# Delta attention: a semaphore for each producer, a place for each step, and waits set again from the data

## The chip, the cores and the metric

The kernel runs on one core of a Trainium2 chip. The metric is the device time of one execution in microseconds. The core has five engines with queues of their own: TensorE (PE), VectorE (DVE), ScalarE (ACT), GpSimd (POOL) and SyncE (SP, which only starts DMAs here). They meet only through semaphores: an instruction raises one when it ends, and another engine's queue, or the same engine's, waits until it has reached a number.

## What is computed

The kernel computes a small model of four layers (attention and feed-forward in each). The change lies in the attention of the first layer, a gated delta rule with 16 heads of 128, two batches and 1,024 tokens:

```python
q = short_conv(x @ Wq.T, conv_q); k = short_conv(x @ Wk.T, conv_k); v = short_conv(x @ Wv.T, conv_v)
v_hat = einsum('bthk,vk->bthv', k, Wsv); e = v_hat - v
s = stack([s_l2, s_l1, s_cos], -1)
beta = sigmoid(_mlp(s, Wb1, bb1, Wb2, bb2)); amp = _mlp(s, Wa1, ba1, Wa2, ba2)
g = -exp(A_log) * softplus(k / norm(k) * amp + dt_bias)
def step(S, inp):
    q_t, k_t, v_t, g_t, b_t = inp
    S = S * exp(g_t)[..., None]
    kv = einsum('bhk,bhkv->bhv', k_t, S)
    delta = (v_t - kv) * b_t[..., None]
    S = S + k_t[..., None] * delta[..., None, :]
    o_t = einsum('bhk,bhkv->bhv', q_t * scale, S)
    return (S, o_t)
o = o * rsqrt(mean(o * o, -1, keepdims=True) + NORM_EPS) * norm_w * sigmoid(x @ Wg1.T @ Wg2.T + bg2)
return o.reshape(Bsz, Tlen, NH * DV) @ Wo.T
```

Here short_conv is a causal convolution over 4 tokens with a silu behind it, and s holds three numbers of how far v_hat is from v.

## The kernel before

`delta_attention` cuts the work into 64 units u: head u // 4, and of the head's 2,048 tokens a group of 512 (`tok`). Units 0 and 1 of a head (`first(u)`) begin the two batches, units 2 and 3 go on with them: they take over three columns of the projections (`tail`) and the state St. A unit passes through the engines like this, by the lines of the kernel before:

- PE projects k, v and q (L301), ACT copies them out scaled by the last tap (L533 the three columns of the tail, L534 the rest), DVE adds the other taps (L723, three times each for k, v and q). In units 2 and 3 of a head three small multiplications `early` (L871), a sum L873 and an addition L876 bring in the tail. ACT puts the silu on all three (L587), DVE rounds tiny numbers away (L860 k, L862 v, L878 q).
- PE turns v (L352), multiplies k by Wsv (L360), ACT and DVE square and multiply (L579 to L581, L621 to L623, L757, L852), PE sums over channels (L345) and turns the sums (L475). DVE takes them out (L750 to L752), POOL takes roots (L685, L686, L687), and the small MLPs run on POOL (L682, L705 to L708, L697, L698), ACT (L570, L636) and DVE (L766 to L770, L787, L832 to L834, L906 to L908). PE spreads their results over the channels (L367, L373), DVE forms z (L845), ACT and DVE the softplus (L626 to L630, L824, L740, L842) and ACT the decay (L574).
- Seven levels lv turn 128 tokens of a chunk into one triangular solve. At each, PE multiplies keys with scaled keys and queries (`products`, L312 for levels 0 to 4, L318 for 5 and 6), POOL scales keys and queries for the next level (`scale`: L666 kq, L667 kF, L668 tot), DVE copies the products under a mask (`mask`, L737), PE multiplies blocks (`in_blocks`, L325), ACT copies the result (Xs, L591) and DVE subtracts it (TB, L886).
- The recurrence goes over 4 chunks k: PE multiplies the state St (L394), DVE forms R (L796), PE multiplies (L433), ACT copies Dl (L607), PE adds up state and output (L463, L467, L470), and DVE renews St (L896 in the first chunk of a batch, L898 in the others).
- The output is squared (ACT L596) and gated (DVE og, L840), PE sums the squares (L508), DVE and POOL make the root (L817, L703), PE multiplies by Wo (L424) and DVE adds to x (L783).

The units overlap. A slot g runs from 0 to 7 x 63 + 33; a step with the offset off works on unit (g - off) / 7 where that is whole (`at`). The order of the `if` blocks in an engine's part, slot after slot, is the order of its queue: it is written out by hand, and an engine carries out its queue strictly in this order. Some ten steps share counters: `scaled`, `masked` and `p_mm` count all seven levels, `rounded` is raised only by the last of three roundings. Where an engine's instruction needs the result of the one ahead of it, `ch.link` (class Chain) puts a wait right behind the producer, so that the next instruction in the queue waits, whichever it is.

## Time and profile before

| | before |
|---|---|
| median of 3 runs | 6105.31 us (6090.98 to 6112.95) |
| span of the profiled execution | 6108.1 us |
| PE busy in it | 5563.4 us, 91% |
| DVE, ACT, POOL busy | 3399.1 us (56%), 2691.6 us (44%), 1937.6 us (32%) |
| first and last power L685 on POOL, 64 in all | 64.6 and 2568.1 us |

The share of busy time is over all nine stages of the program; the stage of this change ends soon after the last L685. A row of a timeline tells when an instruction (or several like it in a row, xN) began and how long it lasted, with, in square brackets, how long its engine had been idle and who ended that. An instruction that begins before its neighbour's end overlaps with it in the engine's pipeline.

### The profile page before, as it was taken

What the parts mean: (1) busy time and instruction counts of PE and PEld (TensorE: products, weight loads), DVE (VectorE), ACT (ScalarE), POOL (GpSimd) and SP (SyncE); (2) the same over time, 40 slices, a digit from 0 to 9 for tenths busy, and PEclk for the clock granted to TensorE, in tenths of its full rate; (3) what the DMA queues carried; (4) which work ended last, traced back from release to release, by engine and by line L of the source; (5) the groups of instructions that cost most, each with busy time, mean ns of one, the idle gap of its engine ahead of it and who ended that gap; (6) DMA issues with size and microseconds to landing.
All of it is one profiled execution on the core that took longest, in us unless ns stands there. A gap on an engine that the chain in (4) does not pass through costs nothing. (4 is left out here: it accounts for less than half of the span.)

```text
span 6108.1 us, 162699 instructions
## 1 busy us (share of the span) xinstructions
PE 5563.4 (91%) x69266; PEld 3711.6 (61%) x69266; DVE 3399.1 (56%) x7451; ACT 2691.6 (44%) x5744; POOL 1937.6 (32%) x2352
## 2 busy tenths in 40 slices
PE   5888888888888888889999999899989899999999
PEld 3666656666665666656777776533336667767665
DVE  5677777777777777633444443386624444444322
ACT  4555555555555555513555553236651222222211
POOL 3666666666666666610000000110000011111000
PEclk7999999999999999979999999989999999999999
DMA  0000000000000000000000000000010112111100
GB/s 28 7 7 7 7 7 7 7 7 7 7 7 3 7 7 7 3 17 12 15 11 11 15 10 23 7 1 1 1 56 1 37 67 67 67 67 67 63 7 7
DMA packets 34317, 116.15 MB, mean 19 GB/s; under 512 B 4416, under 2 KB 9792, under 8 KB 33600
## 3 DMA queue, kind: packets, MB, share of 16 engines
q1 hardware_dynamic: 33600, 105.74, 5.1%
q8 instruction: 553, 9.06, 0.6%
q14 instruction: 164, 1.34, 0.1%
HBM read 103.63 MB, written 2.10 MB: 17 GB/s over the span
## 5 line engine op out<-in xcount | busy, mean ns | idle before, releaser
L666 POOL TENSOR_TENSOR d_kq<-d_kq,d_tot 128x512 f32<-128x512 f32 x448 | 558.6, 1247 | 788.1 <-PE d_lpd L312 635.2
L723 DVE SCALAR_TENSOR_TENSOR d_qkv<-d_fr,d_wts,d_qkv 128x509 f32<-128x509 f32 (+2 forms) x576 | 428.3, 744 | 81.7 <-ACT d_qkv L534 72.6
L301 PE MATMUL d_fr<-xnT,d_wts 128*128 128x512 f32 x768 | 404.0, 652 | 9.4 <-DMA d_wts<-in_headw 5.2
L1845 DVE TENSOR_REDUCE r_nm<-r_ps 128x2 f32<-128x1024 f32 x256 | 307.8, 1223 | 138.7 <-PE r_ps L1664 138.6
L1943 PE MATMUL e_pj<-xnT,e_wts 128*128 128x512 f32 x768 | 347.9, 602 | 13.9 <-DMA e_wts<-in_w3all 12.2
L1059 POOL TENSOR_TENSOR f1rstd<-f1var,mhalf 128x4 f32<-128x4 f32 x4 | 4.0, 1010 | 1090.1 <-DVE f1var L1084 1090.1
L1765 ACT ACTIVATE r_pT<-r_ps 128x512 f32<-128x512 f32 x512 | 274.9, 598 | 146.3 <-PE r_ps L1672 145.8
L667 POOL TENSOR_TENSOR d_kF<-d_kF,d_tot 128x256 f32<-128x256 f32 x448 | 316.8, 707 | 0.0
L1296 PEld LDWEIGHTS c_po<-c_pT,c_vt 128*128 128x128 f32 x2304 | 294.7, 191 | 21.0 <-ACT c_pT L1361 9.3
L1296 PE MATMUL c_po<-c_pT,c_vt 128*128 128x128 f32 x2304 | 301.9, 276 | 0.2
L1664 PE MATMUL r_ps<-r_kT,r_qT 32*128 32x512 f32 x1024 | 291.5, 690 | 2.7 <-DVE r_nm L1845 1.1
L1251 PE MATMUL c_sc<-c_kT,c_qT 128*128 128x512 f32 (+3 forms) x768 | 290.2, 487 | 0.7 <-ACT c_qT L1322 0.7
L1399 DVE TENSOR_TENSOR c_sc<-c_sc,c_mask 128x128 f32<-128x128 f32 x256 | 76.7, 300 | 382.6 <-PE c_sc L1251 382.6
L1672 PE MATMUL r_ps<-r_qT,r_kT 32*128 32x512 f32 x1024 | 278.6, 648 | 0.8 <-ACT r_pT L1765 0.8
L685 POOL TENSOR_TENSOR d_pw<-d_st,d_half 128x20 f32<-128x20 f32 x64 | 250.0, 3907 | 71.5 <-DVE d_sums L752 71.5
L995 PE MATMUL f3pg<-xnT,f3ws 128*128 128x512 f32 x544 | 246.2, 595 | 6.9 <-DMA f3ws<-in_f3w 6.9
L1943 PEld LDWEIGHTS e_pj<-xnT,e_wts 128*128 128x128 f32 x768 | 141.2, 191 | 178.1 <-issue 153.1
L591 ACT ACTIVATE d_Xs<-d_xy 128x128 f32<-128x128 f32 (+1 forms) x384 | 111.3, 290 | 280.6 <-PE d_xy L325 269.4
L534 ACT ACTIVATE d_qkv<-d_fr,d_wts 128x512 f32<-128x512 f32 x192 | 131.8, 686 | 212.8 <-PE d_fr L301 212.0
L433 PE MATMUL d_ca<-d_R,d_TT 128*128 128x128 f32 x512 | 130.6, 339 | 92.7 <-DVE d_R L796 83.9
L301 PEld LDWEIGHTS d_fr<-xnT,d_wts 128*128 128x128 f32 x768 | 138.2, 200 | 125.2 <-issue 104.5
L2074 POOL TENSOR_TENSOR e_acc<-e_acc,e_osq 128x512 f32<-128x512 f32 x60 | 76.1, 1268 | 434.1 <-ACT e_osq L2043 434.1
(437 smaller groups left out, 13527.8 us busy)
## 6 DMA issues: line engine op xcount, KB each, us to landing
e_wts<-in_w3all SPq DMA_DIRECT2D x64, 897.0 KB, 4.6
...
```

Of the source, the lines that this page charges most:

```text
L301: last = nc.tensor.matmul(fr[:, bank, :], w_of(u)[:, w0 + kd * P:w0 + (kd + 1) * P], T.xnT[:, kd, tok(u):tok(u) + GRP], start=(kd == 0), s ...
L666: nc.gpsimd.tensor_tensor(v, v, bc(bc(t_l[:, :, 0], 2, h), 1, 2), ALU.mult)
L667: nc.gpsimd.tensor_tensor(f, f, bc(t_l[:, :, 1], 2, h), ALU.mult)
L685: ch.link(nc.gpsimd.tensor_tensor(pw[:, u % 3], st[:, u % 2], bc(half[:].to_broadcast([P, 5]), 2, NC), ALU.pow))
L723: step = nc.vector.scalar_tensor_tensor(into, fr[:, x // 2, 0:GRP - 3 + i], tap(u, x, i), into, ALU.mult, ALU.add)
L1251: last = nc.tensor.matmul(sc[:, n % 2, k, 0:w], qT[:, h % 2, t * P:(t + 1) * P], kT[:, h // 4 % 2, k * GRP:k * GRP + w], start=True, stop= ...
L1296: last = nc.tensor.matmul(po[:, 0:P], vt[:, n // (4 * QT) % 2, j], pT[:, n % 2, j * P:(j + 1) * P], start=(j == 0), stop=(j == t))
L1664: last = nc.tensor.matmul(ps[:, r + w, :], qT[band(i0 + w), j, tok(t)], kT[band(i0 + w), j // 2, keys], start=True, stop=True, tile_positi ...
L1672: nc.tensor.matmul(ps[:, k, :], kT[band(i), jj // 2, tok(b * QT + kt)], qT[band(i), jj, (G - 1) * GRP:G * GRP], start=True, stop=True, til ...
L1765: nc.scalar.activation(pT[:, N % 3, i, :], ps[:, k, :], ACT.Exp).then_inc(cols_read, 1)
L1845: nc.vector.tensor_reduce(nm[:, t % 2, half, 4 * j + i0:4 * j + i0 + 2], ps[:, row_pair(row - 1):row_pair(row - 1) + 2], AX, ALU.max).then ...
L1943: last = nc.tensor.matmul(pj[:, x % 2, :], w[:, w0 + kd * P:w0 + (kd + 1) * P], T.xnT[:, kd, g * GRP:(g + 1) * GRP], start=(kd == 0), stop ...
```

## The change

The arithmetic stays, and nearly all of the order. Three things change.

The slots become turns: TURNS is 68, and in turn t a step with the offset off (0 to 4) works on unit t - off (`unit`). Each engine's part is one turn of its queue written out, so that each step has a place of its own. PE, POOL and SP keep their order. On DVE the mask of level 1 moves, in units with `early` steps, from behind them to behind the first of them. On ACT the evacuation of k moves ahead of the copy of its tail, in units that have one.

Each producer has its own semaphore, and shared counters go: `scaled_kF[lv]` is raised by L667's successor, `round_k`, `round_v` and `round_q` by the three roundings, `st_floor` by that of L751, `p_mm[lv]`, `yt_mm[lv]` and so on by level. Waits are set anew: one stands where the data needs it and no earlier wait in the queue covers it; many are left only for the first or the last units. Chain has a second form, `did(instruction, name)` and later `after(name)`, which puts the wait ahead of the instruction that needs the result. In the program as built, PE's rows carry 7,353 waits before and 4,316 after, DVE's 7,017 and 4,459, ACT's 4,712 and 3,764, POOL's 1,936 and 1,289. One wait is new: ACT's Abs of sqs 5 waits for the Square that reads it.

The core of the diff:

```diff
+    def did(self, instruction, *step):
         instruction.then_inc(self.sem, 1)
         self.n += 1
+        self.at[step] = self.n
         return self.n
+
+    def after(self, *step):
+        self.need(self.at[step])
 
...
-
-
-def at(g, off):
-    u, r = divmod(g - off, SL)
-    return u if r == 0 and 0 <= u < NU0 else None
+
+
+def unit(t, off):
+    return t - off if 0 <= t - off < NU0 else None
 
```

PE, the transposes of v, the spreads of a1 and rb, and products (of all levels but the first) that wait for kF:

```diff
-                        pe.wait_ge(conv[0], u + 1)
-                        pe.wait_ge(rounded, u + 1)
...
+                        pe.wait_ge(round_v, u + 1)
                         for j in range(NC):
...
+                        pe.wait_ge(rb_ready, u + 1)
+                        for j in range(NC):
+                            last = nc.tensor.transpose(fr[:, 2, ch_(j)], rb[:, j:j + 1].to_broadcast([P, P]), T.ident[:])
+                        last.then_inc(rb_mm, 1)
...
+                    if (u := unit(t, 2)) is not None:
+                        pe.wait_ge(scaled_kF[2], u + 1)
+                        products(u, 3).then_inc(p_mm[3], 1)
```

ACT, the new wait, and k's evacuation; DVE, og, the mask of level 1 and the `early` steps, R of chunk 1; POOL, the scaling:

```diff
+                            act.wait_ge(*w_loaded(u))
+                        act.wait_ge(proj_k, u + 1)
+                        nc.scalar.activation(qkv[:, u % 3, 1], fr[:, 0, :], ACT.Copy, scale=tap(u, 1, 3)).then_inc(evac_k, 1)
+                        if first(u):
+                            if u == 0:
+                                act.wait_ge(tail_set, 1)
+                            nc.scalar.activation(tail[:, u % 2, 1, 0:3], fr[:, 0, GRP - 3:], ACT.Copy).then_inc(tail_k, 1)
...
+                        act.wait_ge(cross_ready, u + 1)
+                        nc.scalar.activation(sqs[:, 2], fr[:, 3, :], ACT.Square)
+                        ch.did(nc.scalar.activation(sqs[:, 3], sqs[:, 5], ACT.Square), "err_sq", u)
+                        ch.after("err_sq", u)
+                        nc.scalar.activation(sqs[:, 5], sqs[:, 5], ACT.Abs).then_inc(err_abs, 1)
...
-                    t_l = tot[:, u % 2, tot_at[lv]:tot_at[lv] + segs].rearrange("p (m two) -> p m two", two=2)
-                    t_n = tot[:, u % 2, tot_at[lv + 1]:tot_at[lv + 1] + segs // 2]
-                    f = even(kF[:, u % 2], h)
...
-                        pool.wait_ge(scaled, 7 * u + lv)
                     v = kq[:, u % 2].rearrange("p x (m two h) -> p x m two h", two=2, h=h)[:, :, :, 1]
-                    nc.gpsimd.tensor_tensor(v, v, bc(bc(t_l[:, :, 0], 2, h), 1, 2), ALU.mult)
-                    nc.gpsimd.tensor_tensor(f, f, bc(t_l[:, :, 1], 2, h), ALU.mult)
-                    nc.gpsimd.tensor_tensor(t_n, t_l[:, :, 0], t_l[:, :, 1], ALU.mult).then_inc(scaled, 1)
...
+                def scale_kF(u, lv):
+                    f = even(kF[:, u % 2], 1 << lv)
+                    return nc.gpsimd.tensor_tensor(f, f, bc(by_pair(u, lv)[:, :, 1], 2, 1 << lv), ALU.mult)
...
+                        ch.did(scale_tot(u, 5), "scaled_tot[5]", u)
+                    if (u := unit(t, 1)) is not None:
+                        pool.wait_ge(st_floor, u + 1)
+                        nc.gpsimd.tensor_tensor(pw[:, u % 3], st[:, u % 2], bc(half[:].to_broadcast([P, 5]), 2, NC), ALU.pow).then_inc(roots, 1)
+                        pool.wait_ge(roots, u + 1)
...
+                        scale_kq(u, 1)
+                        scale_kF(u, 1).then_inc(scaled_kF[1], 1)
+                        ch.did(scale_tot(u, 1), "scaled_tot[1]", u)
+                        ch.after("scaled_tot[1]", u)
...
+                    if (u := unit(t, 4)) is not None:
+                        dve.wait_ge(osq_ready, u + 1)
+                        nc.vector.scalar_tensor_tensor(og[:], tg[:, u % 2], 1.0, co[:], ALU.add, ALU.mult)
...
+                        nc.vector.tensor_scalar(st[:, u % 2, 4], sv[:, 0, :, 0], 1e-24, None, ALU.max).then_inc(st_floor, 1)
...
+                        nc.vector.tensor_tensor(c3(TB[:, 1]), bc(eye[:], 1, NC), c3(xy[:, 0:P]), ALU.subtract)
+                    if (u := unit(t, 0)) is not None:
+                        if not first(u):
+                            nc.vector.tensor_tensor(early[:, :, :, 0], tail[:, u % 2, :, 0:3], bc(taps(u)[:, :, 0], 2, 3), ALU.mult)
+                    if (u := unit(t, 2)) is not None:
+                        dve.wait_ge(p_mm[1], u + 1)
+                        mask(u, 1).then_inc(masked[1], 1)
+                    if (u := unit(t, 0)) is not None:
+                        if not first(u):
+                            nc.vector.tensor_tensor(early[:, :, :, 1], tail[:, u % 2, :, 1:4], bc(taps(u)[:, :, 1], 2, 3), ALU.mult)
+                        if not first(u):
+                            nc.vector.tensor_tensor(early[:, :, :, 2], tail[:, u % 2, :, 2:5], bc(taps(u)[:, :, 2], 2, 3), ALU.mult).then_inc(early_taps[2], 1)
+                        if not first(u):
+                            dve.wait_ge(early_taps[2], n_second(u))
+                            ch.did(nc.vector.tensor_reduce(esum[:], early[:], AX, ALU.add), "early_sum", u)
+                        if not first(u):
+                            ch.after("early_sum", u)
+                            nc.vector.tensor_tensor(qkv[:, u % 3, :, 0:3], qkv[:, u % 3, :, 0:3], esum[:], ALU.add).then_inc(early_added, 1)
...
+                        dve.wait_ge(w_mm[1], u + 1)
+                        nc.vector.scalar_tensor_tensor(R[:, ch_(1)], vtok[:, u % 4, ch_(1)], pw[:, u % 3, 0, 1:1+1], ca[:, 0:P], ALU.mult, ALU.subtract).then_inc(r_ready[1], 1)
```

The queue of DVE in a unit with `early` steps whose St is copied from ca (row L896 before, L955 after), from the second tap of q to the sum of the first MLP; d_qkv, d_early, d_MB and d_St are the tiles qkv, early, MB and St of the code. Before:

```order
L723 SCALAR_TENSOR_TENSOR d_qkv<-d_fr,d_wts,d_qkv 128x511 [waits d_dve_steps]
L857 TENSOR_TENSOR d_TB<-d_eye,d_xy 128x128 [waits d_tr_mm]
L871 TENSOR_TENSOR d_early<-d_tail,d_wts 128x9 [waits d_conv_v,d_conv_k,d_conv_q]
L871 TENSOR_TENSOR d_early<-d_tail,d_wts 128x9 x2
L873 TENSOR_REDUCE d_esum<-d_early 128x9 [waits d_dve_steps]
L876 TENSOR_TENSOR d_qkv<-d_qkv,d_esum 128x3x3 [waits d_dve_steps]
L737 COPY_PREDICATED d_MB<-d_pairs,d_lpd 128x2x32x2 [waits d_p_mm]
L896 COPY d_St<-d_ca 128x128 [waits d_s_mm]
L787 SCALAR_TENSOR_TENSOR d_hid<-d_hid,d_mlp 128x256 [waits d_hid_silu]
L796 SCALAR_TENSOR_TENSOR d_R<-d_vtok,d_pw,d_ca 128x128 [waits d_w_mm,d_dve_steps]
L832 TENSOR_REDUCE d_ba<-d_hid 128x8
```

And the same stretch after:

```order
L793 SCALAR_TENSOR_TENSOR d_qkv<-d_fr,d_wts,d_qkv 128x511 [waits n0centred]
L931 TENSOR_TENSOR d_TB<-d_eye,d_xy 128x128 [waits d_tr_mm]
L934 TENSOR_TENSOR d_early<-d_tail,d_wts 128x9
L800 COPY_PREDICATED d_MB<-d_pairs,d_lpd 128x2x32x2 [waits d_p_mm_1]
L940 TENSOR_TENSOR d_early<-d_tail,d_wts 128x9
L942 TENSOR_TENSOR d_early<-d_tail,d_wts 128x9
L945 TENSOR_REDUCE d_esum<-d_early 128x9 [waits d_early_taps_2]
L948 TENSOR_TENSOR d_qkv<-d_qkv,d_esum 128x3x3 [waits n0centred]
L955 COPY d_St<-d_ca 128x128
L958 SCALAR_TENSOR_TENSOR d_hid<-d_hid,d_mlp 128x256 [waits d_hid_silu]
L961 SCALAR_TENSOR_TENSOR d_R<-d_vtok,d_pw,d_ca 128x128 [waits d_w_mm_1]
L964 TENSOR_REDUCE d_ba<-d_hid 128x8 [waits n0centred]
```

The mask (COPY_PREDICATED, 128x2x32x2) stood behind L876, two places ahead of R, and now stands behind the first of the three multiplications; the other four steps come behind it.

The queue of DVE at the turn of a unit, from the last TB of level 3 to the first reading of the sums; d_lp, d_og and d_TB are lp, og and TB. Before:

```order
L886 TENSOR_TENSOR d_TB<-d_TB,d_xy 128x256 [waits d_yt_mm]
L898 SCALAR_TENSOR_TENSOR d_St<-d_St,d_tot,d_ca 128x128 [waits d_s_mm]
L824 SCALAR_TENSOR_TENSOR d_lp<-d_ez 128x512 [waits d_w_exp,d_ez_ready]
L740 SCALAR_TENSOR_TENSOR d_lp<-d_ezs,d_lp 128x512 [waits d_dve_steps] x2
L840 SCALAR_TENSOR_TENSOR d_og<-d_tg,d_co 128x512 [waits d_tg_ready,d_yo_mm,d_osq_ready,d_dve_steps]
L737 COPY_PREDICATED d_MA<-d_pairs,d_lpd 128x2x8x32 [waits d_out_spread,d_p_mm]
L886 TENSOR_TENSOR d_TB<-d_TB,d_xy 128x256 [waits d_yt_mm]
L750 TENSOR_SCALAR d_st<-d_fr 128x16 [waits d_sT_mm]
```

And after, where n0centred is the semaphore dve_steps (DVE's own chain) in the place of one that an earlier stage gave back:

```order
L1021 TENSOR_TENSOR d_TB<-d_TB,d_xy 128x256 [waits d_yt_mm_3]
L1025 SCALAR_TENSOR_TENSOR d_St<-d_St,d_tot,d_ca 128x128
L809 SCALAR_TENSOR_TENSOR d_lp<-d_ez 128x512
L803 SCALAR_TENSOR_TENSOR d_lp<-d_ezs,d_lp 128x512 [waits n0centred] x2
L820 SCALAR_TENSOR_TENSOR d_og<-d_tg,d_co 128x512 [waits d_osq_ready]
L800 COPY_PREDICATED d_MA<-d_pairs,d_lpd 128x2x8x32 [waits d_out_spread,d_p_mm_5]
L826 TENSOR_TENSOR d_TB<-d_TB,d_xy 128x256 [waits d_yt_mm_4]
L831 TENSOR_SCALAR d_st<-d_fr 128x16
```

The rows are the same; the L824 of before has lost both waits, og (L840, now L820) three of its four, among them that for DVE's own last step, and St and the reading of the sums theirs.

PE from the last products of the state to the next unit's St product; d_fr is the projections' PSUM tile fr, d_a and d_rb are a1 and rb. Before:

```order
L325 MATMUL d_xy<-d_TB,d_Xs 32x32 [waits d_xs_ready]
L325 MATMUL d_xy<-d_TB,d_Xs 32x32 x15
L325 MATMUL d_xy<-d_Xs,d_TB 32x32 x16
L352 MATMUL d_fr<-ident,d_qkv 128x128 [waits d_rounded,d_conv_q]
L352 MATMUL d_fr<-ident,d_qkv 128x128 x3
L360 MATMUL d_fr<-d_qkv,d_wsv 128x512 [waits d_sums_ready,d_khat_ready,d_y_read]
L367 MATMUL d_fr<-ident,d_a 128x128 [waits d_conv_v,d_tg_ready,d_scal_ready]
L367 MATMUL d_fr<-ident,d_a 128x128 x3
L373 MATMUL d_fr<-ident,d_rb 128x128 [waits d_diag_ready,d_y_read]
L373 MATMUL d_fr<-ident,d_rb 128x128 x3
L394 MATMUL d_ca<-d_St,d_kq 128x128 [waits d_s_ready]
```

And after:

```order
L331 MATMUL d_xy<-d_TB,d_Xs 32x32 x16
L331 MATMUL d_xy<-d_Xs,d_TB 32x32 x16
L474 MATMUL d_fr<-ident,d_qkv 128x128 [waits d_round_v]
L474 MATMUL d_fr<-ident,d_qkv 128x128 x3
L476 MATMUL d_fr<-d_qkv,d_wsv 128x512
L483 MATMUL d_fr<-ident,d_a 128x128 [waits d_tg_ready]
L483 MATMUL d_fr<-ident,d_a 128x128 x3
L487 MATMUL d_fr<-ident,d_rb 128x128 [waits d_rb_ready]
L487 MATMUL d_fr<-ident,d_rb 128x128 x3
L492 MATMUL d_ca<-d_St,d_kq 128x128
```

No row has moved; the transposes of v wait for one rounding in place of the last one, the product with Wsv for nothing, the spread of a1 no longer for rb, and the product with St no longer for St.

## Rows read from the trace of the kernel before

**Rows 1.** The page's head: span, and busy time by engine over all stages.

```profile
span 6108.1 us, 162699 instructions
...
PE 5563.4 (91%) x69266; PEld 3711.6 (61%) x69266; DVE 3399.1 (56%) x7451; ACT 2691.6 (44%) x5744; POOL 1937.6 (32%) x2352
```

**Rows 2.** Stretches: engines' busy us (instructions), granted clock, DMA share, GB/s.

```profile
1008.55:1047.38 38.83, 33.03 (x788) 23.45 (x787) 29.44 (x72) 22.83 (x51) 27.02 (x35) 1.00 0.06 18
...
1086.84:1128.02 41.18, 34.70 (x784) 24.81 (x783) 29.20 (x76) 22.52 (x47) 26.15 (x33) 0.92 0.01 3
1128.02:1165.73 37.71, 32.86 (x784) 22.94 (x783) 28.83 (x71) 22.70 (x50) 26.72 (x33) 1.00 0.01 3
...
64.60:2568.10 2503.50, 2142.30 (x48533) 1496.40 (x48533) 1821.43 (x4542) 1411.86 (x3032) 1656.26 (x2068) 0.95 0.02 6
```

**Rows 3.** Waits, 0 to 2600 us: who waited for whom, us in total, times, longest.

```profile
POOL d_kq L666 <- PE d_lpd L312: 621.2, 220, 5.7
...
PEld d_lpd L312 <- POOL d_tot L668: 41.8, 59, 3.2
...
PE d_fr L352 <- DVE d_qkv L878: 18.1, 32, 6.2
```

**Rows 4.** Timeline of DVE and POOL around og, one unit.

```profile
1162.35 1.42 DVE L740 SCALAR_TENSOR_TENSOR d_lp<-d_ezs,d_lp 128x512 f32<-128x512 f32 x2
...
1163.80 0.69 DVE L840 SCALAR_TENSOR_TENSOR d_og<-d_tg,d_co 128x512 f32<-128x512 f32 x1
1164.41 0.72 DVE L737 COPY_PREDICATED d_MA<-d_pairs,d_lpd 128x512 f32<-128x512 int32 x1
...
1165.43 0.14 DVE L751 TENSOR_SCALAR d_st<-d_fr 128x4 f32<-128x4 f32 x1
1165.50 0.15 DVE L752 COPY d_sums<-d_fr 128x12 f32<-128x12 f32 x1
...
1165.73 3.91 POOL L685 TENSOR_TENSOR d_pw<-d_st,d_half 128x20 f32<-128x20 f32 x1 [0.31 <-DVE d_sums L752]
```

**Rows 5.** Timeline of POOL, the end of an MLP and level 0.

```profile
1139.60 0.73 POOL L708 TENSOR_TENSOR d_hid<-d_hid,d_mlp 128x256 f32<-128x256 f32 x1
1140.40 1.61 POOL L666 TENSOR_TENSOR d_kq<-d_kq,d_tot 128x512 f32<-128x512 f32 x1
1141.98 0.84 POOL L667 TENSOR_TENSOR d_kF<-d_kF,d_tot 128x256 f32<-128x256 f32 x1
```

**Rows 6.** Timeline of PE, DVE and POOL, early steps beside St by L898.

```profile
1064.02 0.59 PE L312 MATMUL d_lpd<-d_kq,d_kF 128*32 128x32 f32 x32
...
1064.38 0.32 DVE L871 TENSOR_TENSOR d_early<-d_tail,d_wts 128x9 f32<-128x9 f32 x3
...
1064.71 1.29 POOL L666 TENSOR_TENSOR d_kq<-d_kq,d_tot 128x512 f32<-128x512 f32 x1 [0.78 <-PE d_lpd L312]
1064.73 0.18 DVE L873 TENSOR_REDUCE d_esum<-d_early 128x9 f32<-128x27 f32 x1
1065.06 0.96 DVE L876 TENSOR_TENSOR d_qkv<-d_qkv,d_esum 128x9 f32<-128x9 f32 x1
...
1065.96 0.74 POOL L667 TENSOR_TENSOR d_kF<-d_kF,d_tot 128x256 f32<-128x256 f32 x1
1066.17 0.32 DVE L898 SCALAR_TENSOR_TENSOR d_St<-d_St,d_tot,d_ca 128x128 f32<-128x128 f32 x1
```

**Rows 7.** The same of DVE and PE, early steps beside St by L896.

```profile
1103.40 1.98 DVE L871 TENSOR_TENSOR d_early<-d_tail,d_wts 128x9 f32<-128x9 f32 x3
...
1106.06 0.32 DVE L896 COPY d_St<-d_ca 128x128 f32<-128x128 f32 x1
...
1106.43 0.79 PE L394 MATMUL d_ca<-d_St,d_kq 128*128 128x128 f32 x2 [2.84 <-DVE d_St L896]
```

**Rows 8.** Timeline of ACT, the squares of the error.

```profile
1154.21 0.62 ACT L622 ACTIVATE d_sqs<-d_sqs 128x512 f32<-128x512 f32 x1
1154.73 0.62 ACT L623 ACTIVATE d_sqs<-d_sqs 128x512 f32<-128x512 f32 x1
```

More of the change, by code:

```diff
@@ L170 @@
 NC = GRP // P
-SL = 7
 NU0 = H0 * B * S // GRP
@@ new lines, in _ @@
+                    if (u := unit(t, 4)) is not None:
+                        if u >= NU0 - 1:
+                            pe.wait_ge(ms_ready, u + 1)
+                        pe.wait_ge(diag_ready, min(u + 3, NU0))
+                        pe.wait_ge(khat_ready, min(u + 2, NU0))
+                        for j in range(NC):
+                            last = nc.tensor.matmul(fr[:, 2 + j // 2, (j % 2) * D:(j % 2 + 1) * D], og[:, ch_(j)], wo[:, head(u) % 2], start=True, stop=True)
+                        last.then_inc(yo_mm, 1)
@@ L742, in _ @@
-                for g in range(SLOTS):
-                    ul, lv = divmod(g - LV_AT, SL)
-                    level = 0 <= ul < NU0
-                    uc, k = divmod(g - CHUNK_AT, SL)
-                    chunk = 0 <= uc < NU0 and k < NC
-                    if (u := at(g, ROOT_AT)) is not None:
-                        dve.wait_ge(sT_mm, u + 1)
+                    return nc.vector.copy_predicated(into, bc(mh(level_pairs(lv), h), 1, 2), lpd[:, 0:2 * n].rearrange("p (x m h) -> p x m h", x=2, h=h))
```

1085 lines of the change are left out of this document (574 added, 511 removed).

## The prediction

> **What bounds it now.** I read the page's head first, then the stretches, then the waits, and last the timeline of single units. The whole execution lasts 6108.1 us and TensorE is busy in 91% of it [rows 1], but that is the sum over nine stages. The stage of this change runs 64 units; the POOL power L685, one a unit, starts at 64.60 the first time and at 2568.10 the last time, and in this stretch the busy sums are PE 2142.30, DVE 1821.43, POOL 1656.26 and ACT 1411.86 of 2503.50 us [rows 2]. So no engine is full: a unit's 39.7 us (2503.50 over 63 steps) go to a chain that passes from engine to engine again and again, and what sets the time is how fast one engine's end becomes the next one's start. The waits show the same: POOL alone stood 621.2 us for level products of PE [rows 3]. The granted clock in the stretch is 0.95 of full; three neighbouring units took 38.83 us at 1.00, 41.18 at 0.92 and 37.71 at 1.00 [rows 2]. A unit with part of its time at the lower of the two levels (1.2 in place of 2.4 GHz) is therefore the dear one: 0.92 is 0.16 x 41.18 = 6.6 us at the lower level, for 2.35 to 3.47 us more, about 0.44 us lost for each us spent there.
>
> **What the change does to the path, term by term.** The arithmetic is untouched. What can move is the gap between neighbours.
>
> 1. A wait of DVE on its own last instruction. L740, twice, runs 1162.35 + 1.42 = 1163.77, and L840, which waits for it, starts at 1163.80: 0.03 behind. L737 behind L840 waits for nothing of DVE and starts at 1164.41, where L840 ends at 1164.49: 0.08 ahead [rows 4]. So a wait for the neighbour costs 0.11 us. The change takes it from L840, and behind L840 come L737, L886, L750 to L752 and then L685, which POOL starts 0.08 after L752 has ended. Nothing hides it: 64 x 0.11 = 7.0 us. The Trainium skill ("VectorE: DVE Perf Modes", section "The DRAIN you can't avoid") says that one can't skip the flush by chaining without semaphores and that the semaphore costs nothing extra; by it this term would be 0. The starts in these rows disagree, and the section behind it ("Two Vector instructions with no wait between them") has an instruction that isn't held start earlier.
> 2. POOL. L685 will be released by L751 in place of L752, which starts 0.07 later (1165.43, 1165.50) [rows 4]. L666 behind L708 starts 1140.40 - (1139.60 + 0.73) = 0.07 after its end, while L667, with no wait, starts at 1141.98, 0.03 before L666 has ended at 1142.01 [rows 5]: 0.10 for such a wait, and it goes twice a unit (level 0 behind L708, level 6 behind L687). 0.27 a unit in all. POOL has its long idle time at the other levels, so I take half: 0.135 x 64 = 8.6; bounds 0 and 17.3.
> 3. R of chunk 1 (L796) loses its wait for L787, the same kind of neighbour as in term 1: 0.11, in half of the units, since in the others it waits for PE's L394: 3.5; bounds 0 and 7.0.
> 4. The transposes L352 need only v, and get their own semaphore (L862) in place of the last rounding L878. PE stood 18.1 us at L352, in 32 units [rows 3]. All of it goes, but what follows on PE (L373, L394) meets DVE's results again; I take a little over half, 10. Bounds 0 and 18.1.
> 5. The next level's products wait for L667 and no longer for L668. PE's loads stood 41.8 us for L668, 59 times [rows 3]. L668 of level 0 is the long one, and there PE only comes sooner to L394, which waits for DVE's St: in the unit at 1106.43 it waits 2.84 us [rows 7]. That wait is the cover, so I take 0; without it 41.8 would be the gain.
> 6. The many small waits dropped elsewhere (a second wait ahead of PE's matmuls, of convolutions ahead of L817 and L842, of L827). Not shown one by one; by rows 4 three such neighbours a unit at 0.10 are 19.2 us if all lie on the path, 0 if none. Half: 9.6.
> 7. A cost: L623 now waits for L622 on ACT. Today L623 starts at 1154.73, 0.10 before L622 ends at 1154.21 + 0.62 = 1154.83 [rows 8]. With a wait it starts some 0.03 behind, the step that term 1 shows: 0.13 more for L626, L627, L628 and L630, and for the Xs (L591) and Dl (L607) that PE waits for. 64 x 0.13 = -8.3; bounds 0 (the chunk's Dl comes late for another reason) and -8.3.
> 8. DVE's mask of level 1 moves in between the first and the second `early` multiplication, in the 32 units that have them. They come in two kinds. **Where St is L898:** today the three take 0.32 us from 1064.38, are through before POOL's L666 starts at 1064.71, and only L876 (0.96 us, an op of 9 columns) is held until L666 ends at 1066.00; St starts at 1066.17 [rows 6]. After the change the mask first waits for the products L312 (1064.02 + 0.59 = 1064.61) and runs 0.43 us; the second multiplication then starts about 1065.0, inside L666, and is held until 1066.0; the sum comes behind it, and L876, 0.33 behind the sum as today (1064.73, 1065.06), falls at 1066.4 into L667 (1065.96 + 0.74 = 1066.70). It ends about 1066.75 in place of 1066.02. The mask is already done, which gives back 0.23, so St starts about 1066.65 in place of 1066.17. PE's L394 and all of DVE's queue (L787, R, L832 to L878) are behind it: 0.45 x 16 = -7.2. **Where St is L896:** the first multiplication is already held (the three last 1.98 us), St starts at 1106.06 and PE waits for it [rows 7]. There the mask runs while the next would be held anyway; about 0.14 earlier, +0.14 x 16 = +2.3. Bounds for both: -7.2 - 7 (if the second kind is held once more) and +8.
> 9. ACT's K evacuation ahead of its small tail copy: DVE still waits for the copy where there is one; PE and the loads of weights get fewer conditions, and the weights come a head before their use. All 0, covered by the distance of a head.
>
> The sum: 7.0 + 8.6 + 3.5 + 10 + 9.6 - 8.3 - 7.2 + 2.3 = 25.5 us off. It is made on the profiled execution of 6108.1 us, 2.8 above the median of the runs, 6105.3; I carry it over to the median: 6080. Nothing is put in for the clock. A measurement tells this kernel from no change at about 0.3%, 18 us.
>
> **Rivals.**
> (a) The waits were free: DVE's and POOL's gaps stay when the waits go, or fall into idle time. Then terms 1 to 3 and 6 vanish, and 10 - 8.3 - 4.9 = -3 leaves 6108, no change. For it: POOL's 621.2 us of waiting for PE. Against it: L737's start before L840 has ended. The skill's sentence on the semaphore would give this result. 0.20.
> (b) More of it is on the path: term 5 half real (21), terms 2, 3 and 6 whole (+21.8), L352 whole (+8): 25.5 + 51 = 76, so 6029. For it: the busy sums, all far below the stretch. Against: L394's wait on St. 0.22.
> (c) The other side: TensorE spends more time at the lower level. The stretch has 0.95, so (1 - 0.95) x 2 x 2503.5 = 250 us there. The price is 0.44 us for each us more. When waits ahead of PE go, its short pauses join into longer ones, as the one of 2.84 us ahead of L394 [rows 7], which lies in the unit of 0.92. From 58 us more at the lower level (mean 0.938) the gain of 25.5 is gone, from 100 us more (0.930) it is slower by 0.3%; at 0.925 the time is 6105 + 55 - 25.5 = 6135. Against it: PE's total idle shrinks with the sum. 0.16.
>
> **How the numbers follow.** The forecast has 0.42, for 6080, its own range 6060 to 6097. All gains at their bounds and no cost give 6105 - (7.0 + 17.3 + 7.0 + 18.1 + 41.8 + 19.2 + 8) = 5987; I let the range begin at 6010 and end at 6120, which leaves out the far end of (b) and most of (c). Faster by over 0.3%: four fifths of the forecast and (b), 0.56; slower: (c) and a little of (a), 0.18; the rest, 0.26, within.
>
> **What the profile after would show.** og starts about 0.08 before L740's second run has ended (term 1). L685 starts before DVE's copy of the sums has ended (2). PE's wait at the v transposes for a rounding is gone, or under 3 us (4). The wait for L668 is gone, while PE's wait ahead of the chunk's L394 for St grows by as much (5). L623 starts 0.03 behind L622 (7). In the units of L898 the second multiplication lasts about 1 us and St comes 0.45 later after L857; if it lasts 0.17, term 8 is wrong (8). The mean unit falls from 39.7 to 39.3 us at a granted clock of 0.95; 0.93 or less is (c), 0.96 or more makes the gain larger than the sum.

## The result: 0.6% slower, with more time at TensorE's lower clock

The median of 6 runs after the change is 6138.66 us (6130.92 to 6157.09), that of 6 runs before 6104.96 us (6090.98 to 6122.70). The ratio is 1.006, with a 95% interval from 1.0036 to 1.0085: slower, outside the range that was given, and on the side that had a chance of 0.18.

The page's head of the profiled execution after:

```profile
span 6132.5 us, 159569 instructions
```

Stretches of it: first the one from the first POOL power (L720, the L685 of before) to the last, then two units. Columns as in [rows 2]:

```profile
66.03:2596.47 2530.44, 2169.88 (x48530) 1520.11 (x48530) 1814.12 (x4542) 1416.29 (x3032) 1653.21 (x2067) 0.93 0.02 6
1135.52:1176.09 40.57, 35.17 (x784) 25.17 (x783) 28.40 (x71) 22.91 (x50) 26.40 (x33) 0.92 0.01 3
1176.09:1214.28 38.19, 33.05 (x788) 23.43 (x787) 29.28 (x72) 22.81 (x51) 27.17 (x35) 1.00 0.06 19
```

The stretch is 26.94 us longer than in [rows 2] and its granted clock is 0.93 and no longer 0.95. The two units answer to the last of [rows 2] and the kind of the first. In what follows the four kinds of unit, which come in turn, are called A (the first of [rows 2]: no early steps, St by L898), B (early steps, St by L898), C (early steps, St by L896) and D (no early steps, St by L896). D took 37.71 us at 1.00 and takes 40.57 at 0.92; A took 38.83 and takes 38.19, both at 1.00. Counted over the clock's records, the stretch had 269 us at the lower level (1.2 GHz) before and has 354 after.

Where D lost its clock: the timeline of POOL, DVE and PE in that unit, from the MLP's end to the state product of chunk 1 (L450, the L394 of before).

```profile
1147.12 0.73 POOL L750 TENSOR_TENSOR d_hid<-d_hid,d_mlp 128x256 f32<-128x256 f32 x1
...
1147.81 1.49 POOL L700 TENSOR_TENSOR d_kq<-d_kq,d_tot 128x512 f32<-128x512 f32 x1
1147.83 1.62 DVE L905 TENSOR_TENSOR d_TB<-d_eye,d_MB 128x128 f32<-128x128 f32 x1
...
1153.58 0.32 DVE L955 COPY d_St<-d_ca 128x128 f32<-128x128 f32 x1
...
1154.05 0.77 PE L450 MATMUL d_ca<-d_St,d_kq 128*128 128x128 f32 x2 [2.25 <-DVE d_St L955]
```

POOL goes from L750 to level 0's scaling L700 without a wait, as term 2 said, and starts at 1147.81. DVE's TB0 (L905: eye minus MB, both in SBUF) starts at 1147.83, two hundredths later, and lasts until L700 has ended: 1.62 us where it took 0.29. Everything behind it in DVE's queue comes that much later, St last; PE has nothing else to do by then and stands 2.25 us in one piece ahead of L450. The Trainium skill ("SBUF — State Buffer", section "Who interferes with whom") says that an instruction of DVE with two SBUF inputs contends with one of GpSimd that reads SBUF, and that the order of issue decides who blocks. By that rule, which the rows bear out (1.62 us for 0.29), the 0.10 us that POOL was given are paid by DVE with 1.3.

The clock of the same unit, first from its power to 1153.80, just before that pause ends, and then behind it:

```profile
1135.52:1153.80 18.28, 14.47 (x230) 9.80 (x228) 15.75 (x35) 8.56 (x21) 17.65 (x20) 1.00 0.01 2
1153.90:1160.50 6.60, 6.45 (x143) 5.59 (x144) 3.73 (x15) 5.10 (x9) 2.69 (x5) 0.50 0.01 2
```

It falls from 1.00 to 0.50 at the end of the pause. In 8 of the 15 D units the fall lies there, 18.0 to 18.3 us behind the power; in the kernel before 14 of the 15 have no fall at all.

TB0 and two pauses of PE in the D unit of before (POOL's L666 starts there at 1140.40 [rows 5], behind TB0):

```profile
1140.37 0.29 DVE L775 TENSOR_TENSOR d_TB<-d_eye,d_MB 128x128 f32<-128x128 f32 x1
...
1143.44 0.46 PE L312 MATMUL d_lpd<-d_kq,d_kF 128*32 128x32 f32 x32 [0.96 <-POOL d_tot L668]
...
1145.38 0.49 PE L394 MATMUL d_ca<-d_St,d_kq 128*128 128x128 f32 x2 [0.42 <-DVE d_St L896]
```

The waits of PE for St, in us in total, times and the longest; after, then before:

```profile
PE d_ca L450 <- DVE d_St L955: 83.8, 31, 3.5
...
DVE d_R L961 <- PE d_ca L450: 20.3, 49, 0.8
...
PE d_lpd L318 <- POOL d_kF L704: 14.3, 25, 2.8
...
PE d_ca L450 <- DVE d_St L953: 13.7, 15, 1.4
...
PE d_fr L474 <- DVE d_qkv L971: 11.7, 2, 5.9
```

```profile
PE d_ca L394 <- DVE d_St L896: 51.4, 31, 3.2
...
PE d_ca L394 <- DVE d_St L898: 5.3, 6, 0.9
```

97.5 us (83.8 + 13.7) where 56.7 stood. The 41.8 us for L668 in [rows 3] are those of PE's weight loads, of which 0.9 are left, now for L704; the matmuls themselves waited 31.1 us for L668 and wait 14.3 for L704. So 17 us went from there and 41 came at St. Two waits for a rounding are left at L474, 11.7 us, both in the first units, and in 49 units DVE's R of chunk 1 waits for PE.

Units of kind B, as term 8 foresaw them, here one with full clock:

```profile
910.67 0.17 DVE L934 TENSOR_TENSOR d_early<-d_tail,d_wts 128x9 f32<-128x9 f32 x1
910.80 0.44 DVE L800 COPY_PREDICATED d_MB<-d_pairs,d_lpd 128x128 f32<-128x128 int32 x1
910.84 1.29 POOL L700 TENSOR_TENSOR d_kq<-d_kq,d_tot 128x512 f32<-128x512 f32 x1 [0.78 <-PE d_lpd L318]
911.04 1.11 DVE L940 TENSOR_TENSOR d_early<-d_tail,d_wts 128x9 f32<-128x9 f32 x1
...
912.78 0.34 DVE L953 SCALAR_TENSOR_TENSOR d_St<-d_St,d_tot,d_ca 128x128 f32<-128x128 f32 x1
...
913.17 0.49 PE L450 MATMUL d_ca<-d_St,d_kq 128*128 128x128 f32 x2 [1.40 <-DVE d_St L953]
```

The second multiplication (L940) starts 0.20 us into L700 and takes 1.11 us; PE stands 1.40 us for St (0.90 in the unit of the same number before, at 909.17).

### The profile page after: what moved, and what is told of

Read it like the earlier page. It is cut to its first block and busy times, and to the rows that moved or that the text cites. A ratio compares the mean times of both kernels' runs of the same rounds, so it can differ in the third digit from the quotient of the medians.

```text
span 6132.5 us, 159569 instructions
## 1 busy us (share of the span) xinstructions
PE 5588.9 (91%) x69266; PEld 3731.6 (61%) x69266; DVE 3391.2 (55%) x7451; ACT 2695.0 (44%) x5744; POOL 1935.2 (32%) x2352
## 5 line engine op out<-in xcount | busy, mean ns | idle before, releaser
L700 POOL TENSOR_TENSOR d_kq<-d_kq,d_tot 128x512 f32<-128x512 f32 x448 | 560.7, 1251 | 822.4 <-PE d_lpd L318 680.2
L704 POOL TENSOR_TENSOR d_kF<-d_kF,d_tot 128x256 f32<-128x256 f32 x448 | 312.5, 698 | 0.0
L720 POOL TENSOR_TENSOR d_pw<-d_st,d_half 128x20 f32<-128x20 f32 x64 | 254.9, 3982 | 58.2 <-DVE d_st L833 51.4
L1239 DVE TENSOR_TENSOR f3hid<-f3act,f3side 128x512 f32<-128x512 f32 x68 | 46.8, 688 | 280.8 <-ACT f3act L1160 280.8
L1520 DVE TENSOR_REDUCE c_nmax<-c_sc 128x1 f32<-128x1024 f32 (+7 forms) x256 | 194.0, 758 | 9.0
L1455 ACT ACTIVATE c_oT<-c_po 128x128 f32<-128x128 f32 x256 | 71.0, 277 | 286.0 <-PE c_po L1413 285.9
```

The costliest lines, as they stand in the source:

```text
L700: return nc.gpsimd.tensor_tensor(v, v, bc(bc(by_pair(u, lv)[:, :, 0], 2, h), 1, 2), ALU.mult)
L704: return nc.gpsimd.tensor_tensor(f, f, bc(by_pair(u, lv)[:, :, 1], 2, 1 << lv), ALU.mult)
```

## Experiments

Ratios are to the kernel before on the same chip, with their 95% interval. That kernel took 6118.87 us beside e1 to e4, 6122.20 beside g1 to g4, 6118.29 beside h1 to h4 and 6115.91 beside k1 and k2, where it had taken 6104.96 beside the change: where an expectation starts from 6105 or 6139 us, its microseconds are some 11 to 17 too low for these chips. Times at the lower level are those of the profiled execution, counted over the clock's records. "At full clock" means that a unit's granted clock is 1.00.

**e1, e2, e3: the two places where DVE and POOL meet, put back.** e1 lets POOL wait for L750, as before; e2 puts the mask of level 1 behind the early steps; e3 does both.

```diff
-                        nc.gpsimd.tensor_tensor(hid[:], hid[:], bc(mlp[:, 3], 1, NC), ALU.add)
+                        ch.link(nc.gpsimd.tensor_tensor(hid[:], hid[:], bc(mlp[:, 3], 1, NC), ALU.add))
...
                             nc.vector.tensor_tensor(qkv[:, u % 3, :, 0:3], qkv[:, u % 3, :, 0:3], esum[:], ALU.add).then_inc(early_added, 1)
+                    if (u := unit(t, 2)) is not None:
+                        dve.wait_ge(p_mm[1], u + 1)
+                        mask(u, 1).then_inc(masked[1], 1)
```

> The kernel after, with one wait more: POOL waits for its own L750 (the addition of the MLP's bias) before it goes on to level 0's scaling L700, as the kernel before did. Theory A (whose turn it is between DVE and POOL): in every fourth unit POOL's L700 now starts 0.02 us ahead of DVE's TB0 (L905), which is then held for 1.5 us; x_res, the q taps and St come 1.1 us later after the power, TensorE's idle time gathers in one piece of 2.24 us ahead of L450, and its clock falls to the lower level in units where it stayed full before. The wait puts L700 back by 0.1 us, so TB0 is through first: L905's mean in those units falls from 1.53 to 0.29 us, L450's idle time there under 0.8 us, those units take about 37.7 us instead of 40.6, and the kernel 6139 - 15 x 2.9 = about 6095, between 6085 and 6110. Theory B (the lost time lies in the other engines' waits, ACT's new one and PE's): a wait more on POOL changes nothing or costs 6 us: 6139 to 6145.

> The kernel after, with DVE's mask of level 1 back behind the five early steps in the units that have them. Theory A: in the units whose St is renewed (L953) the second early multiplication no longer starts inside POOL's L700 and is no longer held 1.1 us; St comes 0.45 us sooner, TensorE's idle time ahead of L450 falls from 1.4 to 0.9 us and about half of these units lose their stretch at the lower clock: 16 x 0.45 = 7 us and up to 16 x 3.4 x 0.44 = 24 us, so 6139 - 20 = about 6119, between 6105 and 6135. The units of TB0 stay at 40.6. Theory B (the place of the mask is without effect, since the held time is only shifted): 6139, within 6.

> The kernel after, with both: POOL's wait for L750, and the mask of level 1 behind the early steps. DVE and POOL then meet as in the kernel before, and what is left of the change is its fewer waits and ACT's new one. Theory A: the two effects add up, 6139 - 44 - 20 = about 6075, between 6060 and 6090, which is what the forecast had as the sum without its terms 2 and 8. Theory B: no better than the kernel before, 6105.

Measured: e1 1.0019 (1.0004 to 1.0033), e2 1.0022 (1.0007 to 1.0036), e3 1.0007 (0.9990 to 1.0024). In e1 a unit of kind D, and then its stretches (all, a D, the A behind it):

```profile
1150.19 0.73 POOL L750 TENSOR_TENSOR d_hid<-d_hid,d_mlp 128x256 f32<-128x256 f32 x1
...
1150.88 0.29 DVE L905 TENSOR_TENSOR d_TB<-d_eye,d_MB 128x128 f32<-128x128 f32 x1
1150.99 1.54 POOL L700 TENSOR_TENSOR d_kq<-d_kq,d_tot 128x512 f32<-128x512 f32 x1
65.38:2578.93 2513.55, 2164.44 (x48530) 1505.03 (x48531) 1820.50 (x4542) 1414.83 (x3032) 1657.70 (x2068) 0.93 0.02 6
1138.58:1175.68 37.10, 32.52 (x784) 22.92 (x783) 28.55 (x71) 22.70 (x50) 26.94 (x33) 1.00 0.01 3
1175.68:1217.02 41.34, 36.21 (x788) 25.20 (x787) 29.99 (x72) 22.82 (x51) 27.39 (x34) 0.92 0.06 17
```

L905 is through before L700 starts, and the unit takes 37.10 us at full clock (12 of the 15 do, with 37.1 to 37.6 us): the order was the cause for D. But the A behind it dropped to 0.92 and 41.34 us, and of 15 units of A and of 15 of B (without the first of each) only two of each stayed at full clock; 328 us stayed at the lower level, so the 44 us expected became some 25 (1.006 to 1.0019), and e1 missed its range. In e2 the second multiplication is short again (lowest, median and highest in ns, 32 times):

```profile
L937 DVE TENSOR_TENSOR d_early<-d_tail,d_wts x32: 157/160/167, 101.1 to 2562.0; 128x9 f32<-128x9 f32 x32
```

and 0.4% came back, as expected, though its trace shows little of it: the stretch of e2 is 2521.33 us, 9 shorter than after the change, with 348 us at the lower level for 354. e3 was to add both up and did not: the theory's sum missed it (6075 expected), the ratio is that of the kernel before, and 358 us are at the lower level. Without the first, its D units are seven at full clock with 37.1 us (one 37.28), one of 38.51 us in which L905 is not held, and six like this (DVE and POOL, then the whole and the unit's stretch):

```profile
986.16 1.49 POOL L700 TENSOR_TENSOR d_kq<-d_kq,d_tot 128x512 f32<-128x512 f32 x1
986.33 1.47 DVE L905 TENSOR_TENSOR d_TB<-d_eye,d_MB 128x128 f32<-128x128 f32 x1
65.92:2586.45 2520.53, 2171.67 (x48530) 1510.84 (x48530) 1821.36 (x4542) 1416.59 (x3032) 1660.85 (x2067) 0.93 0.02 6
972.34:1013.17 40.83, 35.60 (x784) 24.54 (x783) 27.93 (x71) 22.93 (x50) 26.53 (x33) 0.92 0.01 3
```

Here L700 is 0.17 us ahead of L905 even with its wait. This unit had 3.4 us at the lower clock from 4.1 us behind its power on, and L905 starts 13.99 us behind the power, for 12.30 in a unit at full clock. The same holds for all six, and for none of the others: a stretch at the lower level ahead of L905 turns the order round, and each of the six has another one 21 us behind its power.

**e4: the kernel before, with nothing but POOL's wait for L708 gone.**

```diff
-                        ch.link(nc.gpsimd.tensor_tensor(hid[:], hid[:], bc(mlp[:, 3], 1, NC), ALU.add))
+                        ch.did(nc.gpsimd.tensor_tensor(hid[:], hid[:], bc(mlp[:, 3], 1, NC), ALU.add))
```

> The kernel before, with one wait less: POOL no longer waits for its own L708 before level 0's scaling L666. Theory A: L666 starts 0.1 us sooner and gets ahead of DVE's TB0 (L775) in units where the two now start 0.03 us apart; L775's mean there goes from 0.3 to 1.5 us and every fourth unit from 37.7 to 40.5: 6105 + up to 43 = about 6140, at least 6120. Theory B (removing a wait can only help or do nothing): 6099 to 6105.

Measured: 1.0061 (1.0042 to 1.0079). One wait a unit, 64 of the 21,018 that the rows of these four engines carry, costs what the whole change costs. Its timeline in a unit of kind D, and its stretch:

```profile
1157.18 0.73 POOL L708 TENSOR_TENSOR d_hid<-d_hid,d_mlp 128x256 f32<-128x256 f32 x1
...
1157.86 1.50 POOL L666 TENSOR_TENSOR d_kq<-d_kq,d_tot 128x512 f32<-128x512 f32 x1
1157.95 1.55 DVE L775 TENSOR_TENSOR d_TB<-d_eye,d_MB 128x128 f32<-128x128 f32 x1
64.79:2613.30 2548.51, 2183.91 (x48531) 1525.93 (x48531) 1821.78 (x4542) 1414.93 (x3032) 1653.92 (x2068) 0.93 0.02 6
```

The stretch is 45 us longer than in [rows 2], with 371 us at the lower level for 269. 102 us more at 0.44 would be 45, all of it. A fit over the units of each kernel (a length for each kind, and a price for a us at the lower level) gives a lower price, an estimate of 0.36 to 0.38 for the kernels before and after and for e4, so about 38 of the 45; the rest may be what the held TB0 costs at any clock.

**g1 to g4: useless work in TensorE's pauses.** The gate product is done more often than needed, into the same bank and before anybody reads it, so that the true one overwrites it: once ahead of L433 in the kinds A and B, where chunk 0 waits 2.0 us for R, and ahead of the true one by kind (the four numbers in the code are for B, C, D and A). g1 is e3 filled, g2 the kernel before, g3 the kernel after (with two products in D), g4 is g1 without those ahead of L433.

```diff
+                        if not first(u) and u + 1 < NU0:
+                            pe.wait_ge(low0_ready, u + 2)
+                            nc.tensor.matmul(fr[:, 1, :], w_of(u + 1)[:, W_G2:W_END], g1T[:, tok(u + 1):tok(u + 1) + GRP], start=True, stop=True)
                         if u >= 2:
                             pe.wait_ge(r_ready[0], n_second(u))
...
+                        for _ in range((1, 2, 0, 0)[u % 4]):
+                            nc.tensor.matmul(fr[:, 1, :], w_of(u)[:, W_G2:W_END], g1T[:, tok(u):tok(u) + GRP], start=True, stop=True)
                         nc.tensor.matmul(fr[:, 1, :], w_of(u)[:, W_G2:W_END], g1T[:, tok(u):tok(u) + GRP], start=True, stop=True).then_inc(tg_mm, 1)
```

> The kernel of e3_both with useless work in TensorE's long pauses: the gate product L416, whose result is overwritten by the same one, is done once more ahead of L433 in units whose chunk 0 waits for R (2.0 us of idle time there), and once or twice more ahead of the true one in units whose first state product L450 waits 0.9 or 2.8 us for St. Nothing of what is computed changes. Theory A (the loss is the clock's: a long pause of TensorE is followed by a stretch at the lower of its two levels): the stage's time at the lower level falls from 358 us of 2520 to under 120, and at 0.44 us for each the kernel takes 6122 - 105 = about 6017, between 5990 and 6060. Theory B (the lower level comes of something else than these two pauses, or the units are longer for another reason): the time at the lower level stays at 300 to 380, and the kernel takes 6120 to 6160, since a product more costs 1 us where it doesn't fit.

> The kernel before with the same useless gate products at the same places. Theory A: its 269 us at the lower level fall under 120; 6105 - 70 = about 6035, between 6010 and 6070. And it is then slower than g1_e3_filled by about 20 us, since the units at full clock of before take 38.79, 39.06 and 37.71 us and those of e3_both 38.19, 38.67 and 37.10. Theory B: 6105 to 6140.

> The kernel after, filled in the same way, and with two products more in the units in which DVE's TB0 is held and L450 waits 2.24 us. Theory A: the 354 us at the lower level fall under 120, and the kernel takes 6139 - 100 = about 6040, between 6010 and 6070: level with g2_before_filled or some 10 us faster, so that with the clock out of the way the change is no loss. Theory B: 6130 to 6170, and slower than g2_before_filled by the 0.6% of the change.

> As g1_e3_filled, but without the product ahead of L433: only the pause ahead of L450 is filled. Theory A1 (the pause ahead of L450 is the one that brings the clock down): as g1, within 15 us. Theory A2 (the two pauses, some 4 us apart, do it together): between g1 and e3_both, about 6060 to 6090.

Measured: g1 0.9942 (0.9923 to 0.9961), g2 0.9989 (0.9975 to 1.0003), g3 0.9909 (0.9891 to 0.9928), g4 0.9979 (0.9960 to 0.9998). Their stretches, in this order:

```profile
65.28:2551.50 2486.22, 2188.83 (x48686) 1501.79 (x48686) 1834.29 (x4542) 1417.13 (x3032) 1665.96 (x2067) 0.96 0.02 6
```

```profile
64.90:2582.20 2517.30, 2201.80 (x48689) 1513.18 (x48689) 1828.97 (x4542) 1412.06 (x3032) 1660.39 (x2068) 0.96 0.02 6
```

```profile
65.84:2518.51 2452.67, 2171.51 (x48747) 1490.31 (x48747) 1840.99 (x4542) 1415.84 (x3032) 1664.20 (x2068) 0.98 0.02 6
```

```profile
65.90:2573.30 2507.40, 2188.92 (x48628) 1509.62 (x48628) 1832.38 (x4542) 1417.11 (x3032) 1664.48 (x2068) 0.94 0.02 6
```

The kernel after, with more work on the engine that is busiest, is 1.5% faster than without (0.9909 against 1.006), as expected. It kept 108 us at the lower level, g1 208, g2 225 and g4 276. g1 and g2 missed what theory A expected; g2 is in the range of theory B and not told from the kernel before. What they left is in good part in D, which they did not fill: 78 us in g2, where the kernel before had 10, and 68 in g1 for 44 in e3. So fewer falls in B and C brought new ones in D, and g2 alone would not have told the theories apart; k1 does. g4 lies between g1 and e3 (theory A2, though it gained less than that expected): the pause ahead of L433 counts beside that ahead of L450.

**h1 to h4: filled more, and two single terms.** h1 is e3 and h2 the kernel after, each with two products ahead of L433 and three in kind C (h1 also one in D, h2 two, as g3). h3 is h2 with ACT's Abs in a slot of its own, h4 is h2 with DVE's wait behind the second softplus factor, so ahead of og.

```diff
-                        ch.did(nc.scalar.activation(sqs[:, 3], sqs[:, 5], ACT.Square), "err_sq", u)
-                        ch.after("err_sq", u)
-                        nc.scalar.activation(sqs[:, 5], sqs[:, 5], ACT.Abs).then_inc(err_abs, 1)
+                        nc.scalar.activation(sqs[:, 3], sqs[:, 5], ACT.Square)
+                        nc.scalar.activation(sqs[:, 7], sqs[:, 5], ACT.Abs).then_inc(err_abs, 1)
...
-                        ch.did(factor(1), "factor[1]", u)
+                        ch.link(factor(1))
```

> As g1_e3_filled, with more useless gate products: two ahead of L433 (1.15 us of idle time were left there), three in place of two in the units with the longest pause ahead of L450 (1.59 left), and one in the units where g1 had none (2.24 us of pause where TB0 was held). g1 still had 208 us at the lower level, g3 108. Theory A: under 100 us, and 6088 - 50 = about 6040, between 6015 and 6065. Theory B (one product too many delays the path by more than the clock gives back): 6085 to 6110.

> As g3_after_filled, with two useless products ahead of L433 and three in the units with the longest pause. Theory A: the 108 us at the lower level fall under 70, 6066 - 15 = about 6050, between 6035 and 6070, and the best of all so far or level with h1. Theory B (what is left comes of the many small products of the levels and their short pauses, which nothing fills): 6060 to 6075.

> As h2_after_filled_more, with term 7 of the prediction undone: ACT's Abs writes a slot of its own (sqs 7) and no longer waits for the Square ahead of it, which reads what it overwrote. Theory A (the step is on the path, 0.13 us a unit): units at full clock 0.10 to 0.13 us shorter, 6 to 8 us in all. Theory B (ACT has room there): the medians of units at full clock stay within 0.03 us.

> As h2_after_filled_more, with term 1 undone: DVE waits for its second softplus factor right behind it, so before og (L820), as the kernel before did. Theory A (0.11 us a unit on the path, all of it): units at full clock 0.10 to 0.12 us longer, 7 us in all. Theory B (the flush can't be skipped, wait or none): og starts at the same distance behind the factor, and the units stay within 0.03 us.

Measured: h1 0.9878 (0.9862 to 0.9893), h2 0.9896 (0.9878 to 0.9913), h3 0.9867 (0.9848 to 0.9886), h4 0.9895 (0.9875 to 0.9914). h1 and h2 (6046.08 and 6053.39 us) came as theory A has it, with 89 and 71 us at the lower level. The whole times of h3 and h4 can't be told from h2's by their intervals; the units below can.

**k1 and k2: the kernel before with h1's products, and all that was good together** (e3, the slot of its own, h1's products).

> The kernel before with the fillers of h1_e3_filled_more: two useless gate products ahead of L433 where chunk 0 waits for R, and one, three, one and none more ahead of the true one, by unit. Theory A (clock): the time at the lower level falls from 225 us in g2 to about 90, and the kernel takes 6119 - 60 = about 6060, between 6045 and 6085; it is then 10 to 25 us slower than h1 (6046), which has the change without terms 2 and 8, and within 15 us of h2 (6053), the filled kernel after. Theory B (the kernel before doesn't profit from fillers as the kernel after does): 6100 to 6130.

> The kernel after with POOL's wait for L750, the mask of level 1 behind the early steps, ACT's Abs in a slot of its own, and the fillers of h1. Terms that add: h1's 6046 less the 0.14 us a unit that h3 showed, 9 us: about 6037, between 6020 and 6045, and level with h3 (6035) or a little faster. If it is slower than 6050, the order in which DVE and POOL meet has changed again and undone it.

Measured: k1 0.9938 (0.9922 to 0.9954), k2 0.9865 (0.9844 to 0.9885); k2's median is 6032.03 us (before beside it 6115.91), h3's 6034.71 (6118.29); both beat the kernel before and the change, and are level with each other. k1 (6078.65 us, 94 us at the lower level) is inside its range: the kernel before, too, gains 0.6% by fillers. But it missed what was expected of it beside h1 and h2: it is 0.6% slower than h1 (10 to 25 us were expected) and 0.4% slower than h2 (within 15 us). In these kernels there are heads whose four units all run at the full clock, not all of the same length (155.02 to 155.48 us in k1, 154.16 to 155.11 in h2). One such head of each, from power to power over four units; k1, its stretch first:

```profile
63.90:2530.20 2466.30, 2197.11 (x48809) 1501.73 (x48809) 1828.75 (x4542) 1410.38 (x3032) 1664.13 (x2068) 0.98 0.02 6
834.61:989.80 155.19, 139.18 (x3155) 96.44 (x3154) 117.71 (x293) 90.24 (x195) 106.93 (x133) 1.00 0.02 7
```

h1, then h2 with its stretch:

```profile
821.99:975.10 153.11, 138.58 (x3154) 95.79 (x3153) 115.97 (x294) 90.71 (x195) 107.79 (x133) 1.00 0.03 7
```

```profile
65.90:2508.10 2442.20, 2196.62 (x48834) 1497.12 (x48834) 1830.11 (x4542) 1414.72 (x3032) 1667.28 (x2067) 0.99 0.02 6
1452.91:1607.08 154.17, 139.72 (x3157) 96.36 (x3156) 116.07 (x293) 90.67 (x195) 107.53 (x133) 1.00 0.02 7
```

h3, h4, and k2:

```profile
1135.63:1289.21 153.58, 139.75 (x3158) 96.33 (x3157) 116.78 (x293) 90.20 (x195) 107.36 (x134) 1.00 0.03 7
```

```profile
1616.29:1770.88 154.59, 139.51 (x3157) 96.40 (x3157) 116.66 (x293) 90.56 (x195) 108.01 (x134) 1.00 0.02 7
```

```profile
1454.94:1607.39 152.45, 138.90 (x3156) 95.98 (x3155) 117.41 (x293) 90.17 (x195) 107.37 (x133) 1.00 0.03 7
```

155.19 us before and 154.17 after: with the clock out of the way the change gains 1.02 us in four units, 16 us in all. h1, the change without its terms 2 and 8, gains 2.08, 33 us. The heads were picked, but the medians of all units at full clock, kind by kind, add up to the same: 155.13 in k1, 154.17 in h2, 153.10 in h1, 153.60 in h3, 154.60 in h4 and 152.46 in k2. (h2 has one filler more in D than h1, k1 and k2; what that does to D's length was not tried by itself.) The whole runs agree: h2 is 25 us shorter than k1 by the medians, of which 23 us less at the lower level are some 10.

The terms add up in k2, at full clock: 153.11 less h3's step of 0.59 (154.17 to 153.58) would be 152.52, and 152.45 is measured. In the whole kernel this brings nothing over h3, since k2's trace has 98 us at the lower level for h3's 48.

## Why the prediction was wrong

The step that failed is the one under the sum, "Nothing is put in for the clock", and behind it term 2, which took an earlier start of POOL for a gain or nothing. The sum of 25.5 us off has its counterpart in a gain of 16 at full clock (h2 beside k1), but the 85 us more at the lower level cost an estimated 31 (at the fitted 0.37) to 37 (at 0.44). That leaves 15 to 21 of the stretch's 26.94 us; the other 6 to 12 are not accounted for, and the gain at full clock was measured with the pauses filled, not in the two kernels themselves.

The rival (c) named the clock and the place, the pause ahead of L394. It did not have the cause: it let the pauses join because waits ahead of PE go, and e4, in which no wait of PE goes, is as slow as the change. Its price of 0.44 us was taken from three units of different kinds, the slow one a C set against A and D; a C at full clock takes 39.59 us in k1 (with its fillers), so the 41.18 of [rows 2] are 1.6 more for 6.6 us, and that the price came near is luck in part. It had 0.16 because I argued that PE's idle time shrinks with the sum. It did not: the stretch less PE's busy time is 361.2 us before and 360.6 after. What changed is how the pauses lie. In the D unit PE's idle time grew from 4.85 to 5.40 us, and the pauses of 0.96 and 0.42 us ahead of L312 and L394 became one of 0.41 and one of 2.25.

Term by term:
- Term 1 (og) is right in place. L820 starts at 1133.67 where L803 ends at 1133.75. The Trainium skill ("VectorE: DVE Perf Modes", section "The DRAIN you can't avoid") says that the semaphore costs nothing extra; the starts with and without the wait, 0.034 us behind the neighbour's end and 0.082 ahead of it, say otherwise here. h4 puts the wait back, and its head takes 0.42 us more than h2's, 0.105 a unit for the 0.11 forecast. But that is a mean, and its size is luck in part: in h4, A, B and C are 0.41, 0.25 and 0.24 longer and D 0.47 shorter, and TB0 lasts over 0.5 us in other kinds (B and C in 14 of 16 units each for 3 and 6, D in 6 of 17 for 16, A in 2 of 15 for 14). So "nothing hides it" was too simple: this wait, too, decides whom POOL meets. The rows of the kernel after:

```profile
1132.33 1.42 DVE L803 SCALAR_TENSOR_TENSOR d_lp<-d_ezs,d_lp 128x512 f32<-128x512 f32 x2
...
1133.67 0.68 DVE L820 SCALAR_TENSOR_TENSOR d_og<-d_tg,d_co 128x512 f32<-128x512 f32 x1
...
1135.29 0.15 DVE L833 TENSOR_SCALAR d_st<-d_fr 128x4 f32<-128x4 f32 x1
...
1135.52 3.99 POOL L720 TENSOR_TENSOR d_pw<-d_st,d_half 128x20 f32<-128x20 f32 x1
```

- Term 2 is wrong, and in its sign. The power does start 0.08 us behind L833 and no longer behind the copy of the sums, so 0.07 sooner, but it lasts 3.99 us for the 3.91 of [rows 4], so nothing comes of it; why, no run tells. L700 behind L750 does start 0.10 us sooner, and that is what gets it ahead of TB0 (e1, e4). The prediction costed it as a gain or nothing; whom POOL would meet 0.1 us sooner wasn't asked.
- Term 3 (R) was not tried by itself. R waits for PE in 49 of the 64 units, so DVE's own wait can have ended last in 15 at most: 1.7 us for the 3.5 forecast.
- Term 4: the wait of 18.1 us at the v transposes is gone but for 11.7 in the first units, more than the 3 forecast. What it was worth by itself was not tried.
- Term 5 is right in that no gain of this size shows and St's wait grew. But the 41.8 us were read from the weight loads, the matmuls had waited 31.1, and St's wait grew by 41 where 17 had gone: most of that is the late St of D (term 2), not the cover.
- Term 6 was not tried by itself; h1's 33 us over k1 stand against 21.8 for terms 1, 3, 4, 6 and 7, and with 1 and 7 as measured (6.7 and -9.4) some 36 us are left for 3, 4, 6 and what no term named, where I had 23.1.
- Term 7 is right, a little too small: L663 starts 0.03 behind L661, and h3 takes it out for 0.59 us in four units, 0.15 a unit for 0.13. Rows of the kernel after:

```profile
1164.63 0.62 ACT L661 ACTIVATE d_sqs<-d_sqs 128x512 f32<-128x512 f32 x1
1165.28 0.63 ACT L663 ACTIVATE d_sqs<-d_sqs 128x512 f32<-128x512 f32 x1
```

- Term 8 is right in its mechanism for kind B: the second multiplication takes 1.11 us, and B at full clock takes 39.16 us in h2 and 38.68 in h1, 0.48 for the 0.45 forecast. It is too small, since nothing was put in for the clock here either: the pause grew from 0.90 to 1.40 us, and B has no unit at full clock after the change, five before and five in e2. e2 gets back 0.4%, 23 us for the 5 net, of which its trace shows 9.

What stays open: which pauses together bring the clock down. No single length parts them: 2.01 us ahead of L433 stood in A of the kernel before, which ran at 1.00 in 11 of 15 units. And e1 and e3 drop in A and B, for which no unit by itself gives a reason but the one before it; what differs there is that PE's pause ahead of L450 in D is 1.00 us in both (the median), in one piece, where the kernel before has 0.42. That this brings the fall was not tried.
